# Graph attention with residual and layer norm: roots apart from scalings on POOL, Q or K ahead of three output projections, V ended in slot 4, transfers that change both quarters each time

## The chip, the core and the metric

The kernel runs on one core of one Trainium2 chip. The metric is the device time of one execution in microseconds (us), lower is better. Of the kernel before there are three timed executions and one profiled execution. "Same" means within 2% of the time before.

## What is computed

Eight batches of 1024 tokens with 384 features; six heads of 64 features; an adjacency matrix masks each score.

```python
q = _heads(x @ Wq + bq); k = _heads(x @ Wk + bk); v = _heads(x @ Wv + bv)
scores = einsum('bhqd,bhkd->bhqk', q, k) / sqrt(64)
probs  = softmax(scores + where(adj, 0.0, -9e15)[:, None], axis=-1)
ctx    = einsum('bhqk,bhkd->bhqd', probs, v)            # heads side by side: 384 features
x      = layernorm(x + (ctx @ Wf + bf), axis=-1)         # eps 1e-5
```

All arithmetic is float32. Projections and scores are made as three products of a high and a low part (`_hi`, `_lo`) of each operand.

## The kernel before

All engines run programs that were written out by hand and meet at semaphores. A batch is 24 **slots**, walked by all engines in the same order; PE (TensorE) may be a slot or more ahead. Slot s makes the scores of two heads for 128 queries: `group` of 256 queries s//6, pair of heads (s%6)//2, half s%2. Two slots fill one **group of probabilities** (12 a batch, numbered 0 to 11; group g is filled in slots 2g and 2g+1), which lies in half g%2 of `prob`.

What happens to a slot and a group:

- PE: `scores`, 12 matmuls (L499) into `score_ps`, as soon as DVE has read the slot before (`masked`).
- DVE (VectorE): `mask_scores` twice (L675, adds the mask and takes the row minimum into `row_min`), then `turn_squares` twice (L682, transposes 32x32 squares of `prob`), after ACT's exponentials. The first mask of a group waits until the transfers of the group two before have landed (`landed`), since they read the same half of `prob`. Then `divide` (L692) if the slot mixed a group, `invert_sums` in odd slots, and for each projected tile `add_residual` (L699) and `moments` (L706 to L716; the last one, L716, is the first guess of an inverse root, `guess_done`).
- ACT (ScalarE): an early eviction if the slot's first job is an "i", two exponentials (L605), then the other evictions. A Q or K job is read twice, as `q_hi`/`k_hi` and as `raw` (L597), which is one of two buffers; the next use of a `raw` buffer waits until POOL has made the low part out of it (`lo_done`).
- SP (SyncE): `move` in odd slots: after the transposes of a group it issues 16 transfers (L306), each of one quarter (32 partitions) of `prob` to one quarter of `prob_t`, 128 KB. The first eight, then a load of `x_in`, a store (`STORES`) and a load of `res` (`RES_LOADS`) if the tables say so, then the other eight, then a load of the adjacency.
- PE: `mix` (L514, 32 records) multiplies a landed group with V into `context_ps`.
- POOL (GpSimd): low parts (`low_part`, L793 and L789), masks out of the adjacency (L771), diagonals (`make_diagonal`, L799), `context_low` (L805), `residual` (L782: adds the bias to the loaded `res`), and `normalise`: 12 dependent operations on 128x2 (L820 to L823: three Newton steps of the inverse root) and then `scale_rows` (two operations on 128x384, L300). In a slot POOL does them in this order: low parts, mask, diagonal, context_low, residual, normalise.

`STEADY` names the jobs of PE in each slot behind the scores, as (kind, index, piece, ahead): "i" spreads inverse sums (L436), "m" mixes a group, "k", "q", "v" project (nine matmuls at L405 to L407), "x" transposes a piece of the next batch's x, "p" projects one tile of 128 tokens out (nine matmuls). A "p" waits until `context_lo` of the third mix of its group of queries is there (`context_lo_done`). The fourth number 1 marks work for the next batch; a negative index is work left from the batch before. Jobs other than "m" rotate over three PSUM banks. `RESIDUALS` and `NORMALISE` give the slots of POOL's work on each of the four groups of 256 tokens; -1 and -2 are the groups 3 and 2 of the batch before. The last batch has two more slots, 24 and 25.

Lines that the prediction speaks of: slot 21 is `[("p", 4), ("k", 1, 0)]`, slot 9 begins with `("p", 0)`, slot 5 is `[("v", 7), ("m", 0)]` where the mix of group 0 waits until the last V is evicted, and `NORMALISE = {0: -2, 8: -1, 12: 0, 18: 1}`.

Of the kernel before, what the change touches and what calls it, by code (L numbers as in the profile page):

```python
# [62 lines left out]

STORES = {1: -2, 9: -1, 13: 0, 19: 1}
RES_LOADS = {2: 0, 10: 1, 14: 2, 20: 3}
X_LOADS = {4: (0, 0), 6: (0, 1), 11: (1, 0), 12: (1, 1)}
RESIDUALS = {6: 0, 13: 1, 17: 2, 23: 3}
NORMALISE = {0: -2, 8: -1, 12: 0, 18: 1}

# [29 lines left out]
def evicted_early(mode, s):  # L99

    jobs = [w for w in slot_work(mode, s) if w[0] != "m"]
    return jobs[:1] if jobs and (jobs[0][0] == "i" or s == 5) else []

# [13 lines left out]
def graph_attention(nc, x, adj, wq, bq, wk, bk, wv, bv, wf, bf, out):  # L117
# [15 lines left out]
    with ExitStack() as ctx:  # L133
# [170 lines left out]
        def move_square(queue, group, a, c):  # L304

            queue.dma_start(prob_t[32 * c:32 * c + 32, group % 2, a].rearrange("p q h n -> p (q h n)"),  # L306
                            prob[32 * a:32 * a + 32, group % 2, c].rearrange("p q h n -> p (q h n)")
                            ).then_inc(landed[group % 2], 16)
# [6 lines left out]
        def _(sp):  # L315
# [26 lines left out]
            def move(b, group, part):  # L342
                if part == 0:
                    sp.wait_ge(squared, at(b, UNITS, 4 * group + 4))
                    sp.wait_ge(mixed, at(b, GROUPS, group + 1))
                for a in (2 * part, 2 * part + 1):
                    for c in range(4):
                        move_square(sp, group, a, c)

# [297 lines left out]
        def _(dve):  # L647
# [71 lines left out]
            def body(b):  # L719
                for s in slots_of(b.mode):  # L720
# [11 lines left out]
                    for job in work:  # L732
                        if job[0] == "p":
                            add_residual(b, job)
                            moments(b, job[1])

            weights = 0
# [27 lines left out]
        def _(pool):  # L765
# [41 lines left out]

            def normalise(b, group):
                pool.wait_ge(guess_done, at(b, 4, group + 1))
# [9 lines left out]
                for _ in range(NEWTON_STEPS):  # L819
# [3 lines left out]
                    result(nc.gpsimd.tensor_tensor(guess, guess, newton[:], ALU.mult))  # L823
                scale_rows(nc.gpsimd, group)

            def body(b):
                for s in slots_of(b.mode):
                    work = slot_work(b.mode, s)
                    for job in work:
# [9 lines left out]
                    for group in contexts_split(b.mode, s):  # L839
                        context_low(b, group)  # L840
                    if s in RESIDUALS:
                        residual(b, RESIDUALS[s])
                    if s in NORMALISE and (NORMALISE[s] >= 0 or b.mode != "first"):
                        normalise(b, NORMALISE[s])
                    if s == SLOTS:
                        normalise(b, 2)
                    if s == SLOTS + 1:
                        normalise(b, 3)

# [35 lines left out]
```

## Time and profile before

| | |
|---|---|
| median of 3 timed executions | 1355.2 us (1343.33, 1355.2, 1359.98) |
| the profiled execution's own time | 1353.83 us |
| its span, first to last instruction | 1352.0 us |
| mean granted clock of TensorE | 0.964 |
| busy: PE, weight loads, DVE, ACT, POOL | 89%, 66%, 78%, 54%, 48% |
| DMA queue of SP, share of 16 engines | 76.7% |

How to read it: PE is busy nearly nine tenths of the span, so the question at each change is which waits of PE it ends and what PE waits for then. An idle engine other than PE costs only where PE waits for it in the end. The timeline rows used below lie in the batch that begins at 346.14 us and ends at 507.96 us, the third of eight; slot numbers are those of that batch. In a timeline row the columns are start (us), length (us), engine, line, operation, what it writes and reads, its shape, how many were merged, and in brackets how long the engine was idle before it and what ended that.

### The profile page before, as it was taken

The numbers are of one execution on the slowest core, as the hardware profiler recorded it, in microseconds if no ns is written. First come the engines' busy times: TensorE is split into PE (matmuls) and PEld (weight loads), VectorE is DVE, ScalarE is ACT, GpSimd is POOL, SyncE is SP. The second block draws the span as 40 slices with busy tenths as digits, with TensorE's granted clock in tenths as the row PEclk, the third lists the DMA queues.
The fourth block names the chain that finished last, engine by engine and source line by source line (L and its number), as shares of the span: only waits on it lengthen the run. The fifth ranks groups of instructions, "written<-read, shape, count | busy, mean of one in ns | idle before, by whom it ended". The sixth has DMA issues, their size and how long they took to land.

```text
span 1352.0 us, 23753 instructions
## 1 busy us (share of the span) xinstructions
PE 1196.9 (89%) x8406; PEld 889.4 (66%) x8406; DVE 1057.4 (78%) x1617; ACT 736.7 (54%) x1404; POOL 654.4 (48%) x958
## 2 busy tenths in 40 slices
PE   7998899888998889888899898998899888998873
PEld 5765677656776667666677666766577666776542
DVE  5788777887778877788777888688877887779881
ACT  5655555555555656466455555555655555554540
POOL 1235562545625555375544664445643555624534
PEclk9999999998999999999898998999999999999987
DMA  4688867788678877788787887789867897678873
GB/s 154 161 190 213 189 159 191 190 221 192 153 190 199 223 181 177 184 207 201 170 199 173 212 191 183 177 188 224 193 152 190 199 228 185 162 170 196 204 185 86
DMA packets 111607, 251.66 MB, mean 186 GB/s; under 512 B 27904, under 2 KB 62336, under 8 KB 111488
## 3 DMA queue, kind: packets, MB, share of 16 engines
q1 hardware_dynamic: 111488, 250.13, 76.7%
q8 instruction: 67, 1.10, 0.4%
q14 instruction: 52, 0.43, 0.1%
HBM read 36.11 MB, written 12.58 MB: 36 GB/s over the span
## 4 chain that ended last, share of the span: by engine, by line
PE 51%; DVE 16%; SPq 11%; ACT 7%; POOL 7%; issue 5%; DMA 3%; POOLq 0%; ACTq 0%; DVEq 0%
PE context_ps L514 14%; PE score_ps L499 12%; SPq L306 10%; PE job_ps L405 8%; DVE prob L682 7%; PE job_ps L406 7%; PE job_ps L407 7%; ACT prob L605 5%; DVE prob L675 5%; DMA prob_t<-prob 2%; PE job_ps L436 2%; POOL res L300 2%; POOL context_lo L805 1%; POOL xt_lo L789 1%; DVE stats L706 1%
## 5 line engine op out<-in xcount | busy, mean ns | idle before, releaser
L675 DVE CUSTOM_DVE_ANT_0 prob<-score_ps,mask 128x1024 f32<-128x1024 f32 x384 | 454.5, 1220 | 169.0 <-PE score_ps L499 141.8
L605 ACT ACTIVATE prob<-prob,row_min 128x1024 f32<-128x1024 f32 x384 | 440.5, 1149 | 210.2 <-DVE row_min L675 210.1
L682 DVE STREAM_TRANSPOSE prob<-prob 128x1024 f32<-128x1024 f32 x384 | 458.5, 1232 | 75.9 <-ACT prob L605 75.9
L514 PE MATMUL context_ps<-prob_t,v_all 128*64 128x256 f32 x3072 | 356.5, 385 | 43.5 <-DMA prob_t<-prob 38.1
L514 PEld LDWEIGHTS context_ps<-prob_t,v_all 128*64 128x64 f32 x3072 | 232.7, 139 | 153.2 <-issue 60.1
L499 PE MATMUL score_ps<-k_hi,q_hi 64*128 64x512 f32 x768 | 141.6, 446 | 16.2 <-DVE row_min L675 16.2
L805 POOL TENSOR_TENSOR context_lo<-context,context_hi 128x256 fp32r<-128x256 f32 x96 | 70.6, 735 | 171.6 <-ACT context_hi L612 171.6
L771 POOL TENSOR_SCALAR mask<-adj_in 128x1024 f32<-128x1024 uint8 x64 | 67.0, 1046 | 170.8 <-DVE row_min L675 157.7
L793 POOL TENSOR_TENSOR q_lo<-raw,q_hi 128x256 fp32r<-128x256 f32 x95 | 69.3, 734 | 164.0 <-ACT raw L597 162.3
L405 PE MATMUL job_ps<-xt_hi,weight_hi 128*128 128x256 f32 (+1 forms) x423 | 143.3, 339 | 0.0
L406 PE MATMUL job_ps<-xt_lo,weight_hi 128*128 128x256 f32 (+1 forms) x423 | 138.4, 327 | 0.0
L407 PE MATMUL job_ps<-xt_hi,weight_lo 128*128 128x256 f32 (+1 forms) x423 | 138.1, 326 | 0.0
L405 PE MATMUL job_ps<-weight_hi,context_hi 128*128 128x384 f32 x192 | 77.1, 402 | 64.0 <-POOL context_lo L805 64.0
L499 PE MATMUL score_ps<-k_lo,q_hi 64*128 64x512 f32 x768 | 121.0, 392 | 0.0
L499 PE MATMUL score_ps<-k_hi,q_lo 64*128 64x512 f32 x768 | 120.5, 390 | 0.0
L612 ACT ACTIVATE context_hi<-context 128x256 fp32r<-128x256 f32 x96 | 40.1, 417 | 126.6 <-DVE context L692 126.6
L793 POOL TENSOR_TENSOR k_lo<-raw,k_hi 128x512 fp32r<-128x512 f32 x46 | 58.3, 1282 | 102.7 <-ACT raw L597 102.7
L300 POOL TENSOR_SCALAR res<-res,mean_var,inv_dev 128x384 f32<-128x384 f32 x64 | 105.0, 1647 | 3.5
L597 ACT ACTIVATE raw<-job_ps,bias_qk 128x256 f32<-128x256 f32 (+1 forms) x141 | 75.9, 538 | 56.2 <-POOL q_lo L793 32.6
L799 POOL TENSOR_TENSOR diag<-ident,inv_sum 128x512 f32<-128x512 f32 x96 | 100.0, 1042 | 10.5 <-DVE inv_sum L687 7.4
L499 PEld LDWEIGHTS score_ps<-k_hi,q_hi 64*128 64x128 f32 x768 | 57.7, 186 | 69.6 <-issue 36.4
L405 PEld LDWEIGHTS job_ps<-xt_hi,weight_hi 128*128 128x128 f32 x423 | 82.9, 196 | 21.3 <-issue 14.2
(72 smaller groups left out, 1700.9 us busy)
## 6 DMA issues: line engine op xcount, KB each, us to landing
prob_t<-prob SPq DMA_DIRECT2D x1536, 128.0 KB, 2.4
res<-in_x_dram SPq DMA_DIRECT2D x32, 384.0 KB, 3.9
out_dram<-res SPq DMA_DIRECT2D x32, 384.0 KB, 2.9
x_in<-in_x_dram SPq DMA_DIRECT2D x30, 384.0 KB, 3.8
adj_in<-in_adj_dram SPq DMA_DIRECT2D x31, 256.0 KB, 3.1
res<-in_x_dram SPq DMA_DIRECT2D x1, 768.0 KB, 6.7
prob_t<-in_L_gnn_Wk_dram SPq DMA_DIRECT2D x1, 576.0 KB, 4.0
prob_t<-in_L_gnn_Wq_dram SPq DMA_DIRECT2D x1, 576.0 KB, 8.1
```

Source lines behind the costliest of these rows:

```text
L300: engine.tensor_scalar(res[:, n, :], res[:, n, :], mean_var[:, group % 2, tile, 0:1], inv_dev[:, group % 2, tile:tile + 1], ALU.subtract, ...
L306: queue.dma_start(prob_t[32 * c:32 * c + 32, group % 2, a].rearrange("p q h n -> p (q h n)"), prob[32 * a:32 * a + 32, group % 2, c].rearr ...
L405: pe.matmul(dst, left_hi, right_hi, start=(t == 0), stop=False)
L406: pe.matmul(dst, left_hi, right_lo, start=False, stop=False)
L407: last = pe.matmul(dst, left_lo, right_hi, start=False, stop=(t == FT - 1))
L499: last[head] = pe.matmul(score_ps[:, head, keys], q_part[rows, pair, q], k_part[rows, pair, keys], start=(n == 0), stop=(n == 2))
L514: last = pe.matmul(context_ps[64 * head:64 * head + 64, 0:GQ], v_all[:, kt, col:col + HS], keys, start=(kt == 0), stop=(kt == TT - 1))
L605: nc.scalar.activation(probabilities(t), probabilities(t), ACT.Exp, scale=-1.0, bias=row_min[:, ring:ring + 1], accum_out=row_sum[:, s // ...
L675: nc.vector.tensor_tensor_reduce(probabilities(t), in_quarters(score_ps[:, head, :]), in_quarters(mask[:, s % 2, :]), 1.0, HUGE, ALU.add, ...
L682: nc.vector.transpose(probabilities(t), probabilities(t)).then_inc(squared, 1)
L793: nc.gpsimd.tensor_tensor(lo, copy[:, 0:width], hi, ALU.subtract).then_inc(lo_done, 1)
L799: nc.gpsimd.tensor_tensor(diag[:], ident[:].unsqueeze(1).to_broadcast([P, 4, P]), inv_sum[:, group % 2, :].unsqueeze(2).to_broadcast([P, 4 ...
```

## The change

- `normalise` is split: `find_root` (the 12 small operations) runs at the head of POOL's slot (`ROOTS`), ahead of the low parts; `scale_rows` stays at the end of the slot (`SCALINGS`), and that of group 1 moves from slot 18 to the end of slot 19. In the last batch the scaling of the last group is done by DVE.
- Slots 9, 15 and 21: the Q or K projection stands ahead of the output projection.
- V: two in slot 2, three in slot 3, three in slot 4; the spread of group 0 moves from slot 4 to slot 5.
- The residual of group 3 moves from slot 23 to slot 2 of the next batch, the load of its `res` from slot 20 to 22, the store of group 1 from slot 19 to 21.
- The 16 transfers of a group are issued along diagonals: each next one has another source quarter and another target quarter. Before, four in a row read the same source quarter.

```diff
 STEADY = {
...
-    5: [("v", 7, 0, 0), ("m", 0, 0, 0)],
+    5: [("i", 0, 0, 0), ("m", 0, 0, 0)],
...
-    21: [("p", 4, 0, 0), ("k", 1, 0, 1)],
+    21: [("k", 1, 0, 1), ("p", 4, 0, 0)],
...
-STORES = {1: -2, 9: -1, 13: 0, 19: 1}
-RES_LOADS = {2: 0, 10: 1, 14: 2, 20: 3}
+STORES = {1: -2, 9: -1, 13: 0, 21: 1}
+RES_LOADS = {2: 0, 10: 1, 14: 2, 22: 3}
 X_LOADS = {4: (0, 0), 6: (0, 1), 11: (1, 0), 12: (1, 1)}
-RESIDUALS = {6: 0, 13: 1, 17: 2, 23: 3}
-NORMALISE = {0: -2, 8: -1, 12: 0, 18: 1}
+RESIDUALS = {2: -1, 6: 0, 13: 1, 17: 2}
+ROOTS = {0: -2, 8: -1, 12: 0, 18: 1, 24: 2}
+SCALINGS = {0: -2, 8: -1, 12: 0, 19: 1, 24: 2}
...
-    return jobs[:1] if jobs and (jobs[0][0] == "i" or s == 5) else []
+    return jobs[:1] if jobs and jobs[0][0] == "i" else []
...
-                for a in (2 * part, 2 * part + 1):
-                    for c in range(4):
-                        move_square(sp, group, a, c)
+                for ahead in (2 * part, 2 * part + 1):
+                    for a in range(4):
+                        move_square(sp, group, a, (a + ahead) % 4)
...
+                    if s == SLOTS + 1:
+                        dve.wait_ge(root_ops, at(b, 4 * ROOT_OPS, 4 * ROOT_OPS))
+                        scale_rows(nc.vector, 3)
...
-                scale_rows(nc.gpsimd, group)
 
             def body(b):
                 for s in slots_of(b.mode):
+                    if s == SLOTS:
+                        residual(b, 3)
+                    if s in ROOTS and (ROOTS[s] >= 0 or b.mode != "first"):
+                        find_root(b, ROOTS[s])
                     work = slot_work(b.mode, s)
...
-                    if s in RESIDUALS:
+                    if s in RESIDUALS and (RESIDUALS[s] >= 0 or b.mode != "first"):
                         residual(b, RESIDUALS[s])
-                    if s in NORMALISE and (NORMALISE[s] >= 0 or b.mode != "first"):
-                        normalise(b, NORMALISE[s])
-                    if s == SLOTS:
-                        normalise(b, 2)
+                    if s in SCALINGS and (SCALINGS[s] >= 0 or b.mode != "first"):
+                        scale_rows(nc.gpsimd, SCALINGS[s])
                     if s == SLOTS + 1:
-                        normalise(b, 3)
+                        find_root(b, 3)
```

POOL in slots 18 to 20 of a middle batch, before: the end of the root of group 1 (three of its 12 operations), the scaling, the low parts of slot 19, the diagonal and low context of slot 20.

```order
L821 TENSOR_TENSOR newton<-newton,var_eps 128x2
L822 TENSOR_SCALAR newton<-newton 128x2
L823 TENSOR_TENSOR inv_dev<-inv_dev,newton 128x2
L300 TENSOR_SCALAR res<-res,mean_var,inv_dev 128x384 x2
L793 TENSOR_TENSOR q_lo<-raw,q_hi 128x256
L793 TENSOR_TENSOR k_lo<-raw,k_hi 128x512 x2
L799 TENSOR_TENSOR diag<-ident,inv_sum 128x512
L805 TENSOR_TENSOR context_lo<-context,context_hi 128x256
```

The same place now (line numbers are four higher for POOL and one higher for L300):

```order
L825 TENSOR_TENSOR newton<-newton,var_eps 128x2
L826 TENSOR_SCALAR newton<-newton 128x2
L827 TENSOR_TENSOR inv_dev<-inv_dev,newton 128x2
L793 TENSOR_TENSOR xt_lo<-raw,xt_hi 128x2x8x32 x2
L803 TENSOR_TENSOR diag<-ident,inv_sum 128x512
L809 TENSOR_TENSOR context_lo<-context,context_hi 128x256
L797 TENSOR_TENSOR q_lo<-raw,q_hi 128x256
L797 TENSOR_TENSOR k_lo<-raw,k_hi 128x512 x2
L301 TENSOR_SCALAR res<-res,mean_var,inv_dev 128x384 x2
L803 TENSOR_TENSOR diag<-ident,inv_sum 128x512
L809 TENSOR_TENSOR context_lo<-context,context_hi 128x256
```

The root went from behind slot 18's low parts to ahead of them, and the scaling from ahead of slot 19's low parts to behind them.

PE in slot 21, before: the last scores, then the output projection of tile 4 (nine matmuls, three shown), then K (nine, three shown).

```order
L499 MATMUL score_ps<-k_hi,q_lo 128x512 x4
L405 MATMUL job_ps<-weight_hi,context_hi 128x384
L406 MATMUL job_ps<-weight_lo,context_hi 128x384
L407 MATMUL job_ps<-weight_hi,context_lo 128x384
...
L405 MATMUL job_ps<-xt_hi,weight_hi 128x512
L406 MATMUL job_ps<-xt_lo,weight_hi 128x512
L407 MATMUL job_ps<-xt_hi,weight_lo 128x512
```

And now:

```order
L500 MATMUL score_ps<-k_hi,q_lo 128x512 x4
L406 MATMUL job_ps<-xt_hi,weight_hi 128x512
L407 MATMUL job_ps<-xt_lo,weight_hi 128x512
L408 MATMUL job_ps<-xt_hi,weight_lo 128x512
...
L406 MATMUL job_ps<-weight_hi,context_hi 128x384
L407 MATMUL job_ps<-weight_lo,context_hi 128x384
L408 MATMUL job_ps<-weight_hi,context_lo 128x384
```

Nine matmuls of K now stand between the scores and the projection that waits for `context_lo`. Slots 9 and 15 change in the same way with nine matmuls of Q (128x256).

## Rows read from the trace of the kernel before

**Rows 1.** The page, busy time of each engine, share of the span, instructions
```profile
PE 1196.9 (89%) x8406; PEld 889.4 (66%) x8406; DVE 1057.4 (78%) x1617; ACT 736.7 (54%) x1404; POOL 654.4 (48%) x958
```

**Rows 2.** Waits over the whole span: waiting <- awaited: us, times, longest
```profile
PE job_ps L405 <- POOL context_lo L805: 64.0, 25, 4.6
...
PE context_ps L514 <- DMA prob_t<-prob: 38.1, 20, 9.0
...
ACT raw L597 <- POOL q_lo L793: 32.6, 7, 4.9
...
DVE prob L675 <- DMA prob_t<-prob: 25.7, 17, 2.7
...
PE context_ps L514 <- ACT v_all L576: 5.4, 8, 0.7
```

**Rows 3.** Timeline of PE, slot 21
```profile
490.43 0.66 PE L405 MATMUL job_ps<-weight_hi,context_hi 128*128 128x384 f32 x1 [4.61 <-POOL context_lo L805]
...
493.44 0.52 PE L405 MATMUL job_ps<-xt_hi,weight_hi 128*128 128x512 f32 x1
...
495.79 0.73 PE L499 MATMUL score_ps<-k_hi,q_hi 64*128 64x512 f32 x4
```

**Rows 4.** Timeline of POOL, slots 18 to 20
```profile
472.68 2.54 POOL L789 TENSOR_TENSOR xt_lo<-raw,xt_hi 128x512 fp32r<-128x512 f32 x2 [2.08 <-ACT raw L595]
...
476.87 0.20 POOL L820 TENSOR_TENSOR newton<-inv_dev 128x2 f32<-128x2 f32 x1
...
480.22 3.28 POOL L300 TENSOR_SCALAR res<-res,mean_var,inv_dev 128x384 f32<-128x384 f32 x2
...
489.56 0.73 POOL L805 TENSOR_TENSOR context_lo<-context,context_hi 128x256 fp32r<-128x256 f32 x1 [1.89 <-ACT context_hi L612]
```

**Rows 5.** Timeline of ACT, slots 19 and 20
```profile
484.23 0.69 ACT L597 ACTIVATE raw<-job_ps,bias_qk 128x512 f32<-128x512 f32 x1 [4.91 <-POOL q_lo L793]
...
485.08 1.15 ACT L605 ACTIVATE prob<-prob,row_min 128x1024 f32<-128x1024 f32 x1
```

**Rows 6.** Timeline of DVE, slot 20
```profile
486.35 2.37 DVE L682 STREAM_TRANSPOSE prob<-prob 128x1024 f32<-128x1024 f32 x2 [3.76 <-ACT prob L605]
```

**Rows 7.** Windows: stretch, length, busy PE, PEld, DVE, ACT, POOL, clock, DMA share, GB/s
```profile
490.43:493.44 3.01, 3.01 (x9) 3.01 (x10) 2.85 (x4) 2.17 (x4) 0.00 (x0) 0.50 0.67 226
503.00:504.69 1.69, 1.69 (x12) 1.69 (x11) 1.58 (x3) 0.49 (x2) 0.74 (x1) 1.00 0.92 209
```

**Rows 8.** Timeline of PE, slot 9
```profile
412.01 0.66 PE L405 MATMUL job_ps<-weight_hi,context_hi 128*128 128x384 f32 x1 [2.56 <-POOL context_lo L805]
...
415.03 0.37 PE L405 MATMUL job_ps<-xt_hi,weight_hi 128*128 128x256 f32 x1
```

**Rows 9.** Timeline of SP, transfers of groups 3 and 5
```profile
402.40 10.04 SPq L306 DMA_DIRECT2D prob_t<-prob  x16
...
429.73 4.96 SPq L306 DMA_DIRECT2D prob_t<-prob  x8
...
435.37 5.62 SPq L306 DMA_DIRECT2D prob_t<-prob  x8
```

**Rows 10.** Timeline of PE, slot 14
```profile
443.26 3.67 PE L514 MATMUL context_ps<-prob_t,v_all 128*64 128x256 f32 x32 [1.74 <-DMA prob_t<-prob]
```

**Rows 11.** Timeline of SP, transfers of group 2
```profile
388.99 11.19 SPq L306 DMA_DIRECT2D prob_t<-prob  x16
```

**Rows 12.** Timeline of PE, slot 8, where group 2 is mixed
```profile
403.81 1.47 PE L514 MATMUL context_ps<-prob_t,v_all 128*64 128x256 f32 x12
```

**Rows 13.** DMA in 429 to 444 us: GB/s in 40 equal slices
```profile
GB/s 319 385 135 4 0 240 197 229 197 186 208 175 273 208 186 186 186 229 139 53 180 352 415 357 317 208 208 208 208 186 175 229 240 208 208 127 115 299 360 437
```

**Rows 14.** The page, DMA issues: count, KB each, us from issue to landing
```profile
prob_t<-prob SPq DMA_DIRECT2D x1536, 128.0 KB, 2.4
```

**Rows 15.** Timeline of POOL at the end of the program
```profile
1345.82 3.28 POOL L300 TENSOR_SCALAR res<-res,mean_var,inv_dev 128x384 f32<-128x384 f32 x2
```

**Rows 16.** Timeline of DVE at the end of the program
```profile
1339.06 0.56 DVE L699 TENSOR_TENSOR res<-job_ps,res 128x384 f32<-128x384 f32 x1 [3.24 <-PE job_ps L407]
```

More of the change, by code:

```diff
@@ L806, in context_low, with find_root @@
                                         ALU.subtract).then_inc(context_lo_done, 1)
-            def normalise(b, group):
+            def find_root(b, group):
                 pool.wait_ge(guess_done, at(b, 4, group + 1))
```

10 rows, old and new, of the table STEADY are left out of this document.

## The prediction

> **What bounds the kernel now.** I read the busy times first: PE is busy 89% of a span of 1352.0 us [rows 1], so about 155 us are PE's idle time or hidden in it, and the rest is work that this change only reorders. Then the waits [rows 2]: what PE waits for longest is `context_lo`, 64.0 us in 25 waits, three a batch; then 38.1 us for transfers that have not landed and 5.4 us for evicted V, 8 times 0.67 us. In the third batch the three waits for `context_lo` are 4.61 us in slot 21 [rows 3], 2.56 us in slot 9 [rows 8], and what is left of 64.0 / 8 = 8.0 us a batch, 0.8 us, belongs to slot 15. Each is a "p" job that stands first behind the scores. Behind the long ones TensorE runs at 1.2 GHz for a while: after 4.6 us of idling the nine matmuls of slot 21's projection took 3.01 us at a granted clock of 0.50, the same nine 1.69 us at 1.00 [rows 7]. Slot 9's nine took 415.03 - 412.01 = 3.02 us too [rows 8].
>
> Why is the low context of slot 20 late? Backwards: `context_lo` at 489.56 [rows 4] waits for the quotient that DVE makes after its transposes; these start at 486.35, 3.76 us after DVE had finished its masks, waiting for ACT's exponentials [rows 6]; these start at 485.08, behind an eviction to `raw` at 484.23 that had waited 4.91 us for POOL's `q_lo` [rows 5]. POOL was inside `normalise` for group 1: root from 476.87, scaling from 480.22 to 483.50 [rows 4], 6.6 us in one piece. ACT's wait of up to 4.9 us shows 7 times [rows 2], once in each batch that prepares a next one.
>
> **The change, part by part,** in that batch.
>
> *Slots 18 to 22.* The root takes 480.22 - 476.87 = 3.35 us. At the head of slot 18 it falls into POOL's 2.08 us of idling ahead of `xt_lo` [rows 4] and makes `xt_lo` at most 3.35 - 2.08 = 1.3 us later; the scaling (3.28) goes behind the low parts of slot 19. So `q_lo` comes 3.28 + 3.35 - 1.3 = 5.3 us earlier, and ACT's 4.91 us wait is gone. The exponentials are then held by DVE's masks, which had ended 3.76 us before the transposes began: transposes, quotient and `context_lo` come some 3.6 us earlier, and slot 21's wait of 4.61 shrinks to 1.0. The nine matmuls of K put ahead of it take 495.79 - 493.44 = 2.35 us [rows 3], more than that. The wait is gone whole: 4.61. With it goes the half clock: 3.01 - 1.69 = 1.3 for the projection and some 0.2 at the head of K, whose first matmul is still a slow one (0.52) [rows 3]. Together 6.1 us. What is queued behind the moved root is `xt_lo`, and PE's second K of slot 19 waits for it; it would be ready just as PE comes, so up to 0.5 us could be lost. I take 6.0.
>
> *Slot 9.* Nine matmuls of Q (128x256, half as wide as K, so about 1.2 us) fill part of the 2.56 us; `context_lo` itself hangs on DVE and does not come earlier. The rest, 1.3 us, stays. If the clock then stays at 2.4 GHz (my choice: an idling of 1.3 us instead of 2.56), another 1.3 is saved: 2.5. But slots 12 to 18 run at the pace of the transfers: the mix of group 5 waits for its landing [rows 10], and so does DVE's next mask, 25.7 us in 17 waits [rows 2]. That pace starts with group 5's transposes in slot 11, which come earlier by about 2.2, and group 4's landing lets through 1.5 to 2. I take 1.9.
>
> *Slot 15.* Q ahead hides the 0.8 us, but the next mix waits for group 6's landing, and it will wait that much longer: 0. What ends last there is the two-group loop transposes, 16 transfers, landing, mask.
>
> *V.* The last V is evicted a slot before the mix that needs it: 0.67 a batch [rows 2]. Slot 5's scores come some 1.2 us later: one V in (nine matmuls of 384 columns, 1.7 us as in [rows 7]), one spread out (four records of 256 columns, an eighth of the mix's 3.67 us [rows 10]). Group 2's transfers, issued from 388.99 to 400.18 [rows 11], land 2.4 us after the last issue's start [rows 14], at 402.0, and were mixed at 403.81 [rows 12]: slack 1.9 against 1.2 + 0.67. Just hidden; at worst 0.5 a batch is given back.
>
> *Moved residual, store and load.* The residual leaves POOL between slots 23 and 0, where the root now comes first; both fit before the first `q_lo` of slot 0. The store now stands in group 10's issues and not in group 9's: 0.6 us of SP's queue is moved. 0 in a middle batch.
>
> *Diagonal transfers.* 16 issues take 10.04 us [rows 9], 0.63 each, when SP is not held; a transfer lands 2.4 us after issue [rows 14]. Group 5 took 443.1 - 429.73 = 13.4 us to land, against 15 x 0.63 + 2.4 = 11.85. The issue pace stays, so only the 1.5 us of hold-up can go, in the three or four groups of a batch that PE and DVE wait for, and half of each counts, since a loop spans two groups: bounds 0 and 2.5 us a batch, 0 and 20 in all. While only these transfers run, the engines are 0.92 busy at 209 GB/s [rows 7]; the loads of x go through at 352 to 437 GB/s [rows 13], so something halves them. The targets alternated already, and that did not help, and the hold-up begins behind loads that the order does not touch. I take the low end, 0.3 a batch.
>
> The Trainium skill (SBUF — State Buffer, "Door 1: The DMA port swizzle") says that partitions 0 to 63 share eight of 16 ports and 64 to 127 the others, so a quarter reaches half the ports; by that, alternating halves could let two transfers run side by side, the case of the second rival. The same page ("Can I just issue two DMAs to hit both halves?") speaks against it: two such transfers gained only 6%. The trace has no pair that shows which.
>
> *Last batch.* No next batch, so the slot 18 to 22 term is absent. It keeps 1.9 of slot 9, some 1 to 2 from the store that leaves group 9's issues in a tail paced by landings, and at the very end DVE scales in POOL's place: two operations of at most 0.56 [rows 16] for 3.28 [rows 15], 2.1 saved. I take 6.
>
> **Sum.** 6.0 + 1.9 + 0.67 + 0.3 = 8.9 a batch, seven batches 62, and 6 for the last: 68. Less 2 for group 2's landing (0.3 a batch): 66. The profiled execution took 1353.8 us, so 1353.8 - 66 = 1288; it stands 1.4 below the median of the three runs, which themselves lie 17 us apart, so it is also the median's forecast within that spread.
>
> **Rivals.**
>
> *A. Half of it.* Another wait takes the place of slot 21's: `xt_lo` behind the late root holds K and with it ACT, so POOL's part brings nothing and only K's 2.3 us and Q's 1.2 are filled in, with half the clock's loss: 0.67 + 1.2 + 2.3 + 0.7 = 4.9, times 7, plus 4: 38, which gives 1316. For it: the root cannot start before the first guess, and DVE makes that only after slot 17's transposes. Against it: POOL idled 2.08 us right there. Chance 0.14.
>
> *B. The transfers' order pays as well.* Landings at their best, 2.5 a batch: 20 more, less the 2 already counted: 1270. Chance 0.13.
>
> *C. Slower.* Transfers that mix source and target quarters get in each other's way. A batch now takes 161.8 us for 12 groups, 13.5 each (507.96 - 346.14, the batch's bounds); with one or two other issues a group, a transfer of 0.63 would have to become 0.80 before the queue alone holds the old pace, and at 0.85 a batch is 12 x 14.4 = 173 us, 8 x 11.6 = 93 us more in all: 1447. For it: the engines are 0.92 busy already. Against it: each transfer alone touches the same quarters as before. Chance 0.03.
>
> *D. Within 2%.* Waits for landings grow to eat all but 20 us: 1334. Slots 12 to 18 show that PE's gains can be eaten so; against it, the 6.0 lie in slots 19 to 22, where groups 8 and 9 land with microseconds to spare. Chance 0.06.
>
> The forecast itself has 0.64, with 1276 to 1304 as its own range (last value of each term at its bounds, and the before runs' spread). 8 in 10 reaches into A and B: 1266 to 1314. A measurement tells 2% (27 us) from nothing; faster means below 1328. That takes in the forecast, B and nearly all of A: 0.64 + 0.13 + 0.12 = 0.89; within 2%: the rest of A and D, 0.08; slower 0.03.
>
> **What would show it.** Right: no wait of PE for `context_lo` in slot 21, 1.3 us in slot 9, none in slot 15 with the wait for the landing in slot 16 longer by as much; ACT's wait for `q_lo` gone; the total of that wait down from 64.0 to about 10 to 15 us; none for V; mean clock up. 16 issues still 10 us. Wrong: a wait of PE or ACT for `xt_lo` in slot 19 (A); 16 issues and landing near 11.9 in groups 5 to 7 (B); issues over 0.63 each with no load near (C).

## The result and the profile after

The changed kernel takes 1287.2 us (median of four executions, 1280.7 to 1288.7), the kernel before, in the same rounds, 1350.6 us (1343.3 to 1360.0): a ratio of 0.952, with a 95% interval of 0.945 to 0.958. In a second comparison below it was 1283.6 against 1349.6, again a ratio of 0.952. One of the six executions there, at a granted clock of 0.844, took 1339.5 us and is left out of both numbers. The profiled execution of the changed kernel took 1280.7 us, 6 below its median, and that of before 1353.8, some 3 above: what the two traces differ by (73 us) is more than the change is worth (63 us by the medians).

The page of the changed kernel: busy time of the engines, where [rows 1] answers, and the row on DMA issues, where [rows 14] answers.

```profile
PE 1177.3 (92%) x8406; PEld 867.3 (68%) x8406; DVE 1057.7 (83%) x1619; ACT 737.2 (58%) x1404; POOL 655.1 (51%) x956
...
prob_t<-prob SPq DMA_DIRECT2D x1536, 128.0 KB, 2.4
```

Its waits over the whole span, where [rows 2] answers (waiting <- awaited: us, times, longest).

```profile
PE context_ps L515 <- DMA prob_t<-prob: 39.8, 26, 3.6
...
DVE prob L676 <- DMA prob_t<-prob: 20.5, 16, 3.0
...
PE job_ps L437 <- DVE res L700: 12.8, 14, 1.4
PE job_ps L406 <- POOL context_lo L809: 12.5, 9, 1.9
```

PE's wait for the low context went from 64.0 us in 25 waits to 12.5 in 9. There is no row left for V nor for ACT's wait for `q_lo`. PE's busy time fell by 20 us with the same 8406 matmuls: fewer of them run at half the clock (mean granted clock 0.986 instead of 0.964). The wait for landed transfers stayed where it was, 39.8 us after 38.1.

PE in slot 21 of the third batch, which begins at 325.64 us in this trace; [rows 3] is the same place before.

```profile
462.25 0.51 PE L406 MATMUL job_ps<-xt_hi,weight_hi 128*128 128x512 f32 x1
...
464.48 0.33 PE L406 MATMUL job_ps<-weight_hi,context_hi 128*128 128x384 f32 x1
...
466.14 0.73 PE L500 MATMUL score_ps<-k_hi,q_hi 64*128 64x512 f32 x4
```

POOL in slots 18 to 21, where [rows 4] answers.

```profile
446.73 0.19 POOL L824 TENSOR_TENSOR newton<-inv_dev 128x2 f32<-128x2 f32 x1
...
450.06 2.55 POOL L793 TENSOR_TENSOR xt_lo<-raw,xt_hi 128x512 fp32r<-128x512 f32 x2
...
454.25 0.75 POOL L797 TENSOR_TENSOR q_lo<-raw,q_hi 128x256 fp32r<-128x256 f32 x1
...
457.76 3.29 POOL L301 TENSOR_SCALAR res<-res,mean_var,inv_dev 128x384 f32<-128x384 f32 x2
...
462.50 0.73 POOL L809 TENSOR_TENSOR context_lo<-context,context_hi 128x256 fp32r<-128x256 f32 x1 [0.45 <-ACT context_hi L613]
```

DVE's transposes of slot 20, where [rows 6] answers, and the window of slot 21's projection, where [rows 7] answers.

```profile
459.28 2.39 DVE L683 STREAM_TRANSPOSE prob<-prob 128x1024 f32<-128x1024 f32 x2 [0.16 <-ACT prob L606]
```

```profile
464.48:466.14 1.66, 1.66 (x12) 1.41 (x10) 1.50 (x4) 1.66 (x5) 0.00 (x0) 1.00 0.76 178
```

The root now runs ahead of `xt_lo`, `q_lo` is made before the scaling, and the transposes wait 0.16 us for ACT instead of 3.76. The low context is ready at 462.50 + 0.73 = 463.23 us, the projection that needs it starts at 464.48, behind K: 1.25 us in hand where 4.61 were missing. Its nine matmuls run at a granted clock of 1.00, in 1.66 us instead of 3.01.

Where the time went, stretch by stretch, is read from the starts of each slot's scores on PE, as means over the second to the seventh batch (worked out from the traces, us). The other kernels are those of the experiments below. Each column is one execution, so differences of a few tenths a batch are not sure; that of the changed kernel is one of its fastest, that of before one of its slower ones.

| slots | before | after | x1_rows | x3_same_halves | z1_p_first_9 | y1_one_piece | y3_before_split | y4_before_order |
|---|---|---|---|---|---|---|---|---|
| 0 to 9 | 61.66 | 60.75 | 61.14 | 61.12 | 60.82 | 60.86 | 61.75 | 61.87 |
| 9 to 10 | 8.60 | 6.38 | 6.38 | 6.38 | 7.96 | 6.39 | 7.68 | 6.39 |
| 10 to 15 | 31.21 | 32.13 | 34.94 | 34.81 | 30.33 | 32.37 | 31.44 | 32.30 |
| 15 to 18 | 16.97 | 15.61 | 15.57 | 15.75 | 17.03 | 15.80 | 17.14 | 16.78 |
| 18 to 22 | 32.34 | 26.69 | 26.71 | 26.67 | 26.17 | 29.26 | 27.27 | 28.38 |
| 22 to next | 12.17 | 12.17 | 12.17 | 12.18 | 12.17 | 12.51 | 12.18 | 12.48 |
| batch | 162.95 | 153.73 | 156.91 | 156.91 | 154.48 | 157.19 | 157.46 | 158.20 |

Before to after: 0.9 up to slot 9, 2.2 in slot 9, 0.9 given back up to slot 15, 1.4 up to slot 18, 5.7 up to slot 22. The first batch went from 159.4 to 147.2 us, the last from 191.9 to 185.0.

### The profile page after: what moved, and what is told of

The parts are those of the page before. It is cut to its first block, busy times and chain, and to the rows that moved or that the text cites. A ratio compares the mean times of both kernels' runs of the same rounds, so it can differ in the third digit from the quotient of the medians.

```text
span 1278.9 us, 23768 instructions
## 1 busy us (share of the span) xinstructions
PE 1177.3 (92%) x8406; PEld 867.3 (68%) x8406; DVE 1057.7 (83%) x1619; ACT 737.2 (58%) x1404; POOL 655.1 (51%) x956
## 4 chain that ended last, share of the span: by engine, by line
PE 53%; SPq 16%; DVE 16%; ACT 5%; issue 4%; DMA 3%; POOL 2%; DVEq 0%; POOLq 0%
PE context_ps L515 17%; SPq L307 15%; PE score_ps L500 13%; PE job_ps L406 7%; DVE prob L683 7%; PE job_ps L408 6%; PE job_ps L407 6%; ACT prob L606 5%; DVE prob L676 5%; DMA prob_t<-prob 3%; PE job_ps L437 2%; DVE res L700 1%; DVE stats L707 1%; POOL xt_lo L793 1%; SPq L370 1%
## 5 line engine op out<-in xcount | busy, mean ns | idle before, releaser
L515 PE MATMUL context_ps<-prob_t,v_all 128*64 128x256 f32 x3072 | 359.8, 388 | 40.0 <-DMA prob_t<-prob 39.8
L515 PEld LDWEIGHTS context_ps<-prob_t,v_all 128*64 128x64 f32 x3072 | 236.0, 140 | 151.3 <-issue 58.6
L500 PE MATMUL score_ps<-k_hi,q_hi 64*128 64x512 f32 x768 | 140.7, 444 | 10.5 <-DVE row_min L676 9.7
L407 PE MATMUL job_ps<-xt_lo,weight_hi 128*128 128x256 f32 (+1 forms) x423 | 135.5, 320 | 0.0
L408 PE MATMUL job_ps<-xt_hi,weight_lo 128*128 128x256 f32 (+1 forms) x423 | 135.5, 320 | 0.0
L301 POOL TENSOR_SCALAR res<-res,mean_var,inv_dev 128x384 f32<-128x384 f32 x62 | 101.9, 1650 | 0.0
L406 PEld LDWEIGHTS job_ps<-xt_hi,weight_hi 128*128 128x128 f32 x423 | 79.5, 188 | 32.3 <-issue 25.9
L797 POOL TENSOR_TENSOR k_lo<-raw,k_hi 128x512 fp32r<-128x512 f32 x46 | 58.8, 1288 | 74.5 <-ACT raw L598 74.4
L581 ACT ACTIVATE context<-job_ps 128x256 f32<-128x256 f32 x96 | 37.0, 386 | 95.4 <-PE job_ps L437 75.4
L408 PEld LDWEIGHTS job_ps<-xt_hi,weight_lo 128*128 128x128 f32 x423 | 79.6, 188 | 6.6
```

Source lines behind the costliest of these rows:

```text
L301: engine.tensor_scalar(res[:, n, :], res[:, n, :], mean_var[:, group % 2, tile, 0:1], inv_dev[:, group % 2, tile:tile + 1], ALU.subtract, ...
L406: pe.matmul(dst, left_hi, right_hi, start=(t == 0), stop=False)
L407: pe.matmul(dst, left_hi, right_lo, start=False, stop=False)
L408: last = pe.matmul(dst, left_lo, right_hi, start=False, stop=(t == FT - 1))
L500: last[head] = pe.matmul(score_ps[:, head, keys], q_part[rows, pair, q], k_part[rows, pair, keys], start=(n == 0), stop=(n == 2))
L515: last = pe.matmul(context_ps[64 * head:64 * head + 64, 0:GQ], v_all[:, kt, col:col + HS], keys, start=(kt == 0), stop=(kt == TT - 1))
```

## The experiments

Three comparisons, each on one chip with the kernel before beside it: 1349.6, 1348.1 and 1349.6 us. "After" is the changed kernel. How far a kernel lies from it is taken from the difference of the two ratios (0.001 is 1.35 us), since the kernels of the second and third comparison do not stand beside it; an interval of a ratio is 2 to 5 us to either side, so that a distance under 5 us is not shown.

### The order of the transfers

**x0_after_again** is the changed kernel unchanged, as the mark for the next three.

> The changed kernel as it is, on this job's chip, as the yardstick for the three others of the job. Both theories: the same ratio to the kernel before as measured already, 0.952, so 4.8% less.

Measured: 1283.6 us, ratio 0.952 (0.948 to 0.956).

**x1_rows**: the changed kernel with the old order of transfers.

```diff
-                for ahead in (2 * part, 2 * part + 1):
-                    for a in range(4):
-                        move_square(sp, group, a, (a + ahead) % 4)
+                for a in (2 * part, 2 * part + 1):
+                    for c in range(4):
+                        move_square(sp, group, a, c)
```

> The changed kernel with the transfers in the old order: four in a row read the same source quarter. My theory (the pace of SP's issues and the loads ahead set the landing, the order gives 0.3 us a batch): 2 to 4 us slower than the changed kernel, under 0.3%. Rival B (the order pays, up to 2.5 us a batch): 10 to 20 us slower, 0.8 to 1.6%, with the groups 5 to 7 landing 0.5 to 1.5 us later after their first issue. Issues stay 0.63 us apart in both.

Measured: 1299.5 us, ratio 0.963 (0.960 to 0.967): 15 us more than the mark. The order was worth far more than I gave it.

**x2_alternate**: each next transfer reads from the other half of the partitions (quarters 0 and 1 are one half, 2 and 3 the other). The writes change halves at six of the seven steps in the first eight and at five of seven in the other eight.

```diff
-                for ahead in (2 * part, 2 * part + 1):
-                    for a in range(4):
+                for ahead in (0, 2) if part == 0 else (1, 3):
+                    for a in (0, 2, 1, 3):
                         move_square(sp, group, a, (a + ahead) % 4)
```

> The changed kernel with transfers that change the half of the partitions (quarters 0 and 1 against 2 and 3) each time, sources 0, 2, 1, 3 and targets in step. If the halves are what matters (two transfers in flight then always use different halves), landings behind a load come earlier than with the diagonals: 3 to 8 us faster than the changed kernel. If the issue pace alone matters: within 2 us of it.

Measured: 1284.5 us, ratio 0.951 (0.947 to 0.954): 2 us below the mark by the ratios, 1 above it by the medians. No difference is shown, and the 3 to 8 us expected of it did not come.

**x3_same_halves**: eight in a row read from one half, and four in a row write to one half.

```diff
-                for ahead in (2 * part, 2 * part + 1):
-                    for a in range(4):
-                        move_square(sp, group, a, (a + ahead) % 4)
+                for c in ((0, 1), (2, 3)):
+                    for a in (2 * part, 2 * part + 1):
+                        for to in c:
+                            move_square(sp, group, a, to)
```

> The changed kernel with the worst order by halves: eight transfers read from one half, four in a row also write to the same half. If the halves matter: slower than the old order of rows, 5 us or more over the changed kernel, with more issues held over 0.65 us. If the issue pace alone matters: within 2 us of the old order.

Measured: 1310.6 us, ratio 0.971 (0.968 to 0.974): 26 us more than the mark, 10 more than x1_rows.

The place where it shows is group 5, whose landing the mix in slot 14 waits for. In the third batch, SP's issues around it and the mix, first of the changed kernel. (SP's rows: start, length, what is issued, how many. [rows 9, 10] are the same before.)

```profile
406.04 0.60 SPq L364 DMA_DIRECT2D res<-in_x_dram  x1
406.73 4.95 SPq L307 DMA_DIRECT2D prob_t<-prob  x8
...
420.24 3.67 PE L515 MATMUL context_ps<-prob_t,v_all 128*64 128x256 f32 x32 [2.41 <-DMA prob_t<-prob]
```

The same of x1_rows.

```profile
410.86 5.72 SPq L307 DMA_DIRECT2D prob_t<-prob  x8
...
425.82 4.54 PE L515 MATMUL context_ps<-prob_t,v_all 128*64 128x256 f32 x20 [3.15 <-DMA prob_t<-prob]
```

Of x3_same_halves.

```profile
410.96 5.32 SPq L307 DMA_DIRECT2D prob_t<-prob  x8
...
427.75 4.54 PE L516 MATMUL context_ps<-prob_t,v_all 128*64 128x256 f32 x20 [4.96 <-DMA prob_t<-prob]
```

And of x2_alternate.

```profile
410.67 4.95 SPq L307 DMA_DIRECT2D prob_t<-prob  x8
...
424.27 3.67 PE L515 MATMUL context_ps<-prob_t,v_all 128*64 128x256 f32 x32 [2.49 <-DMA prob_t<-prob]
```

From the group's first issue to the start of its mix: 13.5 us (420.24 - 406.73) after, 15.0 in x1_rows, 16.8 in x3_same_halves, 13.6 in x2_alternate. From the first issue to the last landing, as means of the second to the seventh batch: 13.6, 15.4, 16.0 and 13.4. The kernels below that keep the diagonal order have 13.6 to 14.6 there, so the two slow orders lie outside what one order gives from one execution to the next. In a late landing PE idles longer, and the mix that follows more often runs at the low clock. The window of that mix in x1_rows shows it.

```profile
425.82:432.44 6.62, 6.62 (x34) 4.03 (x34) 4.76 (x6) 2.38 (x4) 0.98 (x1) 0.55 0.95 256
```

It takes 6.62 us at a granted clock of 0.55, against 3.67 at 1.00 for the same 32 records in the changed kernel. Over the six batches the mix of group 5 starts 1.9 us later in x1_rows (96.44 against 94.57 from the batch's start) and takes 1.3 longer (6.09 against 4.77): the 3.2 us a batch of the table, part landing and part clock. By the ratios it is 15 / 8 = 1.9 a batch, since the profiled execution of the changed kernel was one of its fastest.

Which part of the order counts? Counted by halves, in x1_rows, x3_same_halves, after and x2_alternate the longest run of reads from one half is 8, 8, 2 and 1, that of writes to one half 2, 4, 2 and 2, and the times follow: 1299.5, 1310.6, 1283.6, 1284.5. So do the issues that took longer than 0.65 us, 88, 99, 78 and 69 of 1536. By this count runs of reads of 2 instead of 8 bring 15 us, and runs of writes of 4 instead of 2 cost 10. That the targets count is shown: x3_same_halves reads one quarter only twice in a row, where x1_rows reads it four times, and is slower all the same. That reads count by the half and not by the quarter is not shown: no run changes the source quarter each time and stays in one half.

The Trainium skill (SBUF — State Buffer, "Door 1: The DMA port swizzle") gives a reason for counting by halves, eight ports for each; these four runs agree with it, but no view shows the ports. Its other sentence there, that two DMAs on both halves gain only 6% ("Can I just issue two DMAs to hit both halves?"), tells nothing of sixteen queued ones behind other loads: here the landing of group 5 moved from 16.0 to 13.4 us with their order.

### Slots 18 to 22

**y1_one_piece**: root and scaling together again, at the end of slots 0, 8, 12 and 18.

```diff
-                    if s in ROOTS and (ROOTS[s] >= 0 or b.mode != "first"):
-                        find_root(b, ROOTS[s])
                     work = slot_work(b.mode, s)
...
-                    if s in SCALINGS and (SCALINGS[s] >= 0 or b.mode != "first"):
-                        scale_rows(nc.gpsimd, SCALINGS[s])
+                    if s in ROOTS and (ROOTS[s] >= 0 or b.mode != "first"):
+                        find_root(b, ROOTS[s])
+                        scale_rows(nc.gpsimd, ROOTS[s])
```

> The changed kernel with root and scaling in one piece at the end of slots 0, 8, 12 and 18, as before; all else as changed. My theory (the piece of 6.6 us in slot 18 holds ACT's eviction and through it exponentials, quotient and low context by 3.6 us): ACT waits some 4.9 us for q_lo in slot 19 again, slot 21's projection waits 2.4 us (3.6 less the 1.2 us that it has in hand behind K), so 2.4 to 4 us a batch with the slow clock, 17 to 28 us in all, 1.3 to 2.2% slower than changed. Rival (the reordering of K and p alone carries the gain): within 5 us of changed.

Measured: 1307.6 us, ratio 0.971 (0.967 to 0.975): 25 us more than x0_after_again. Of the 3.5 us a batch in the table 2.6 lie in slots 18 to 22. Its waits, and slot 21 of the third batch.

```profile
ACT raw L598 <- POOL q_lo L797: 32.8, 7, 5.0
...
PE job_ps L406 <- POOL context_lo L809: 27.2, 18, 2.3
```

```profile
468.20 0.69 ACT L598 ACTIVATE raw<-job_ps,bias_qk 128x512 f32<-128x512 f32 x1 [4.96 <-POOL q_lo L797]
...
474.40 0.66 PE L406 MATMUL job_ps<-weight_hi,context_hi 128*128 128x384 f32 x1 [2.34 <-POOL context_lo L809]
```

ACT's seven waits are back (32.8 us in all against 32.6), and with K ahead 2.34 us of the 4.61 remain in slot 21. The chain POOL, ACT, DVE, POOL, PE is shown.

**y2_p_first_21**: the changed kernel with the projection ahead of K in slot 21 again.

```diff
-    21: [("k", 1, 0, 1), ("p", 4, 0, 0)],
+    21: [("p", 4, 0, 0), ("k", 1, 0, 1)],
```

> The changed kernel with the output projection ahead of K in slot 21, as before. My theory: the low context is there 1.0 us after the scores end, so PE waits 1.0 us in slot 21 and nothing more: 7 us slower than changed, 0.5%. Rival (K's place carries the gain): the wait is 3 us or more and the clock falls, 25 us or more slower.

Measured: 1293.9 us, ratio 0.960 (0.956 to 0.963): 10 us more than x0_after_again. The wait in slot 21 is 1.03 to 1.05 us in each of the six middle batches; the prediction had it at 1.0. The nine matmuls behind it take 1.80 to 1.82: no half clock after any of these short waits. In its trace slots 18 to 22 take 27.88 us, 1.2 more than in the changed kernel; another 1.4 a batch lies in slots 10 to 15, at the landing of group 5, which this edit does not touch.

**y3_before_split**: the kernel before with the root apart from the scaling and the moved residual, store and load, and nothing else.

```diff
-STORES = {1: -2, 9: -1, 13: 0, 19: 1}
-RES_LOADS = {2: 0, 10: 1, 14: 2, 20: 3}
+STORES = {1: -2, 9: -1, 13: 0, 21: 1}
+RES_LOADS = {2: 0, 10: 1, 14: 2, 22: 3}
...
-RESIDUALS = {6: 0, 13: 1, 17: 2, 23: 3}
-NORMALISE = {0: -2, 8: -1, 12: 0, 18: 1}
+RESIDUALS = {2: -1, 6: 0, 13: 1, 17: 2}
+ROOTS = {0: -2, 8: -1, 12: 0, 18: 1, 24: 2}
+SCALINGS = {0: -2, 8: -1, 12: 0, 19: 1, 24: 2}
```

> The kernel before with only roots and scalings apart, and the residual, store and load of group 3 and 1 moved as changed; orders of PE's jobs and transfers as before. My theory: ACT's wait in slot 19 gone, slot 21's wait from 4.6 to 1.0 us and no half clock behind it: 5 us a batch, 35 us less than before (2.6%). Rival A (root at the head holds xt_lo, nothing gained by POOL's part): within 7 us of before.

Measured: 1316.4 us, ratio 0.977 (0.974 to 0.979): 31.6 us less than before. It is POOL's part, with the residual, store and load that moved along. Its waits:

```profile
PE job_ps L406 <- POOL context_lo L806: 40.1, 25, 2.6
...
PE context_ps L515 <- ACT v_all L577: 5.4, 8, 0.7
```

The waits for the low context fell from 64.0 to 40.1, 24 us in seven batches or 3.4 each (4.61 became about 1.0), and the longest is now 2.6, the one in slot 9. Of the 5.5 us a batch in the table 5.1 lie in slots 18 to 22 and 0.9 in slot 9, which this kernel does not touch (see the last section).

**y4_before_order**: the kernel before with Q or K ahead in slots 9, 15 and 21, and nothing else.

```diff
-    9: [("p", 0, 0, 0), ("q", 0, 2, 0), ("x", 0, 0, 1)],
+    9: [("q", 0, 2, 0), ("p", 0, 0, 0), ("x", 0, 0, 1)],
...
-    15: [("p", 2, 0, 0), ("q", 1, 3, 0)],
+    15: [("q", 1, 3, 0), ("p", 2, 0, 0)],
...
-    21: [("p", 4, 0, 0), ("k", 1, 0, 1)],
+    21: [("k", 1, 0, 1), ("p", 4, 0, 0)],
```

> The kernel before with only the Q or K projections ahead in slots 9, 15 and 21. My theory: slot 21's wait of 4.6 shrinks by K's 2.3 us with part of the slow clock, slot 9 brings 1.9, slot 15 nothing: 4.5 to 5.5 us a batch, 32 to 40 us less than before (2.4 to 3%). If it and y3 both give 35, their sum is more than the 62 that both together brought, since the wait in slot 21 is gone but once.

Measured: 1325.1 us, ratio 0.984 (0.981 to 0.987): 22.9 us less than before, and less than expected. (The profiles differ by 30 us; that of before is one of its slower executions.) In the table slot 9 gives its whole 2.2, but slots 10 to 15 take 1.1 of it back, and the last batch is 2.6 us longer than before. PE's waits show where it went. The first row is the low context, the second the landing.

```profile
PE job_ps L405 <- POOL context_lo L805: 27.2, 18, 2.3
```

```profile
PE context_ps L514 <- DMA prob_t<-prob: 55.4, 30, 9.0
```

36.8 us less for the low context, 17.3 more for landings than in [rows 2].

### Slots 9, 15, 12 and 18, and V

**z1_p_first_9**: the changed kernel with the projection first in slot 9 again.

```diff
-    9: [("q", 0, 2, 0), ("p", 0, 0, 0), ("x", 0, 0, 1)],
+    9: [("p", 0, 0, 0), ("q", 0, 2, 0), ("x", 0, 0, 1)],
```

> The changed kernel with the output projection ahead of Q in slot 9. My theory: PE waits 2.6 us instead of 1.3, and the clock falls again for the projection (1.3 us), but only 1.9 us a batch of these 2.6 reach the end since slots 12 to 18 go at the pace of the transfers: 15 us slower than changed, 1.2%. Rival (the transfers' pace swallows it all): within 4 us. Rival (all of it counts): 20 us.

Measured: 1288.5 us, ratio 0.955 (0.953 to 0.957), 3.5 us more than x0_after_again, with overlapping intervals; at 1.9 a batch it should have been 15. PE's two waits in the third batch:

```profile
390.38 0.41 PE L406 MATMUL job_ps<-weight_hi,context_hi 128*128 128x384 f32 x1 [2.55 <-POOL context_lo L809]
...
420.32 3.67 PE L515 MATMUL context_ps<-prob_t,v_all 128*64 128x256 f32 x32 [1.88 <-DMA prob_t<-prob]
```

The changed kernel has 1.29 us at the first place.

```profile
390.79 0.41 PE L406 MATMUL job_ps<-weight_hi,context_hi 128*128 128x384 f32 x1 [1.29 <-POOL context_lo L809]
```

So slot 9's wait is doubled, as it should be, and slot 10 starts 1.65 us later (means of the six batches). But the mix of group 5 starts only 0.94 later, and it ends 0.16 earlier, because it takes 3.67 us in all six batches instead of a mean of 4.77. From slot 15 to 18 the kernel loses 1.4, mostly in a wait for group 6 (1.23 instead of 0.13), and by the batch's end 0.75 is left. What slot 9 saves is taken back at the landings of groups 5 and 6, part as a wait, part as the low clock behind it.

**z2_p_first_15**: the same for slot 15.

```diff
-    15: [("q", 1, 3, 0), ("p", 2, 0, 0)],
+    15: [("p", 2, 0, 0), ("q", 1, 3, 0)],
```

> The changed kernel with the output projection ahead of Q in slot 15. My theory: PE waits about 0.9 us for the low context, and the wait for group 6's landing in slot 16 is shorter by as much: within 3 us of changed. Rival: 0.9 us a batch, 7 us slower, if group 6 has landed by the time PE comes.

Measured: 1288.9 us, ratio 0.954 (0.951 to 0.957): 3 us more, with overlapping intervals. Next to nothing, as the prediction had it.

**z3_v_as_before**: V in slots 2 to 5 as before, the spread of group 0 in slot 4.

```diff
-    2: [("i", -1, 0, 0), ("m", -1, 0, 0), ("v", 0, 0, 0), ("v", 1, 0, 0)],
-    3: [("v", 2, 0, 0), ("v", 3, 0, 0), ("v", 4, 0, 0)],
-    4: [("v", 5, 0, 0), ("v", 6, 0, 0), ("v", 7, 0, 0)],
-    5: [("i", 0, 0, 0), ("m", 0, 0, 0)],
+    2: [("i", -1, 0, 0), ("m", -1, 0, 0), ("v", 0, 0, 0)],
+    3: [("v", 1, 0, 0), ("v", 2, 0, 0), ("v", 3, 0, 0)],
+    4: [("i", 0, 0, 0), ("v", 4, 0, 0), ("v", 5, 0, 0), ("v", 6, 0, 0)],
+    5: [("v", 7, 0, 0), ("m", 0, 0, 0)],
...
-    return jobs[:1] if jobs and jobs[0][0] == "i" else []
+    return jobs[:1] if jobs and (jobs[0][0] == "i" or s == 5) else []
```

> The changed kernel with V in slots 2 to 5 and the spread of group 0 in slot 4, as before. My theory: the wait of 0.67 us for the last V is back in each of 8 batches and group 2 has a microsecond more in hand: 4 to 5 us slower than changed, 0.4%. Rival: less than 2 us, if the earlier V was paid for by a later landing of group 2.

Measured: 1292.1 us, ratio 0.957 (0.954 to 0.960): 7 us more, 0.9 a batch; the ends of the two intervals still overlap. The eight waits are back.

```profile
PE context_ps L515 <- ACT v_all L577: 5.4, 8, 0.7
```

**z4_q_first_11_17**: a step further on the same path. In slots 12 and 18 of the changed kernel PE waits for DVE to read the projection out of its bank (12.8 us in 14 waits), so Q goes ahead in slots 11 and 17 too.

```diff
-    11: [("p", 1, 0, 0), ("q", 1, 2, 0), ("x", 2, 0, 1)],
+    11: [("q", 1, 2, 0), ("p", 1, 0, 0), ("x", 2, 0, 1)],
...
-    17: [("p", 3, 0, 0), ("q", 2, 3, 0), ("x", 0, 1, 1)],
+    17: [("q", 2, 3, 0), ("p", 3, 0, 0), ("x", 0, 1, 1)],
```

> The changed kernel with Q ahead of the output projection in slots 11 and 17 as well. The next spread (slots 12 and 18) waits 0.65 and 1.3 us for DVE to read the projection's bank, three jobs back; with Q three jobs back it waits for ACT instead. If ACT is done by then: these waits go, 1.3 us of slot 18 counts (the mix of group 7 has landed), 0.65 of slot 12 does not (group 4 lands later): up to 10 us faster than changed, 0.8%. If the transposition of x behind it then waits for the same bank: within 2 us.

Measured: 1288.4 us, ratio 0.955 (0.953 to 0.956), no gain. PE's waits:

```profile
PE context_ps L515 <- DMA prob_t<-prob: 45.0, 24, 4.0
...
PE job_ps L416 <- DVE res L700: 2.5, 6, 0.4
```

The wait for DVE is nearly gone (2.5 us), and the wait for landings has grown from 39.8 to 45.0. It is the same lesson as in slot 9.

## Why the prediction came out right

The forecast was 1288 us and a gain of 66; measured were 1287.2 and 63.4. The total is right, but two of its terms were wrong and cancel: slot 9 stood (1.9 - 0.4) x 8 = 12 us too high, the order of the transfers (1.9 - 0.3) x 8 = 13 us too low. Nothing in the prediction tied the one to the other, so it is luck that the sum holds.

**Slots 18 to 22: right, 6.0 a batch.** The table has 5.65. The two ways of undoing it (25 us for POOL's part, 10 for PE's) add up to 35 us, 5 for each of seven batches. That is less than 5.65 since the two cover each other: without POOL's part 2.3 us of wait are left, without K 1.05, together 3.4 of the 4.61. The steps came as worked out: ACT's wait gone, 1.0 us left in slot 21 without K ahead, none with it, and the projection at the full clock. Two small costs were there as well: PE waits a mean 0.10 us for `xt_lo` in slot 19, for which up to 0.5 had been allowed, and 1.26 instead of 0.78 in slot 18 for DVE's read of a bank.

**Slot 9: the step that failed is how much group 4's and 5's landings let through.** The local saving was exactly as predicted: 1.29 us of wait left and full clock, 2.2 of 2.5 us in the stretch. But of the 1.9 that was to survive, z1_p_first_9 finds 3.5 / 8 = 0.4 a batch (0.75 in its profiled execution). Not 15 us, but 3.5, and even that is not clear of nothing. PE now waits a mean 0.59 us in slot 12 for group 4's landing, where before it waited for none, and 2.49 instead of 2.22 in slot 14 for group 5's. The prediction saw that slots 12 to 18 go at the transfers' pace and then took the upper end of what they would let through. It also missed the second way in which an early arrival at a late landing costs: after idling for 2.1 to 3.3 us ahead of the mix of group 5, PE ran it at the low clock in four of six batches (5.2 to 5.4 us instead of 3.67), before, after 1.7 to 2.9 us, in two of six. How long it idles does not decide it alone: the two at full speed came behind 2.41 and 3.30 us.

**The diagonal order: the term was 0.3 a batch, and it is 1.9.** 15 us by the ratios, three quarters of rival B's 20. The bounds of 0 and 2.5 held it; the choice of the low end was the error. Both reasons for it fail. "The targets alternated already, and that did not help" said nothing on the sources, and x3_same_halves shows that the alternating targets did help: without them it is 10 us worse. "The hold-up begins behind loads that the order does not touch" is true of where it begins, not of how long it lasts. And the change itself made the place tighter. SP's load of `res` before:

```profile
426.87 0.58 SPq L363 DMA_DIRECT2D res<-in_x_dram  x1
```

From its end, 426.87 + 0.58 = 427.45, SP stood still until group 5's first issue at 429.73 [rows 9], as a mean of six batches for 2.16 us; now it goes on from 406.04 + 0.60 = 406.64 at 406.73, directly behind the load. In the old order such a group takes 15.4 us to land in x1_rows and 14.4 in y4_before_order, instead of the 13.9 it took before, in the new one 13.6. So the two wrong terms belong together. In x1_rows the stretch from slot 10 to 15 is 3.7 us longer than before and eats nearly all that slots 0 to 9, 9 and 15 had saved (0.5 + 2.2 + 1.4 = 4.1); with the new order it is 0.9 longer. So the new order takes back most of what the earlier arrival costs at that landing; the saving of slot 9 itself it lets through only in small part, as z1_p_first_9 shows. What the order would be worth without the change of slot 9 is not known: no run has the old order, slot 9 as before and the rest as changed.

**V: right.** 0.67 a batch predicted, 0.9 measured, with an uncertainty as large (z3_v_as_before). The eight waits of 0.67 us are gone, and group 2's landing gave no new wait of PE in slot 8, so the 2 us set aside for it were not needed.

**Slot 15: right in size, wrong in detail.** Worth 0 predicted, 3 us measured, with overlapping intervals. The wait taken away was a mean 1.0 us rather than 0.8, in part since slot 21's 4.61 in the third batch is above its mean of 4.35. And the wait in slot 16 did not grow by as much: it fell, from a mean of 0.75 us to 0.13, since the slow mix of group 5 had already used up the time (in z1_p_first_9, where that mix is never slow, it is 1.23).

**Last batch:** 6 predicted, 191.9 - 185.0 = 6.9 in the profiles. **The base:** the sum started from the profiled 1353.8 us, while the medians of before in three further comparisons are 1348.1 to 1349.6. So the base was 3 us too high, and so was the gain, 66 against 63; this too cancels in the 1288.

**The rivals.** A did not happen: ACT does not wait for `xt_lo`, and PE only the 0.10 us in slot 19. B's worth came by three quarters, but not its sign: groups 5 to 7 land 13.6, 13.1 and 12.8 us after their first issue, not 11.9. Against the 13.9, 14.2 and 12.8 of before that is little; what the order is worth shows only beside x1_rows, since the other parts of the change had made the landings harder. D's mechanism, landings that eat what PE gains, is real, but with the old order it eats some 4 us a batch and leaves slots 18 to 22 alone, so that x1_rows still gains 50 us. C is refuted: an issue still follows the one before it after 0.63 us (sixteen with no load among them take 10.6 us on average, before 10.5) and the landings of groups 5 and 6 come sooner.

## What to carry to other kernels

Where a stage goes at the pace of transfers, price a saving ahead of it at nothing until something makes the landing itself earlier; test it by putting the wait back, not by reading that the wait is gone. A helper engine's long job should be split so that the part that others wait for goes first, and the whole chain behind the delay counted back to the bound engine: that was worth half of this change. And the order in which equal transfers are queued is free to choose: let no long run of them read from one half of the partitions, or write to one. Here that was worth a quarter of the change.

## What the runs showed of the hardware that was not expected

- **The order of quarter transfers alone moves this kernel by 26 us**, 1284.5 to 1310.6, at the same median issue pace of 0.63 us and the same bytes. Most of the difference comes between slots 10 and 15, at groups 4 to 6, among or just ahead of whose transfers loads of x and `res` stand; groups 8 and 9 land in 11.7 to 13.5 us in each of the four orders.
- **The same wait does not always bring the low clock.** Slot 9's projection after 2.55 us of idling, in the second to the eighth batch, took over 2.9 us in four of seven before, in two of seven in z1_p_first_9, in one of seven in y3_before_split, and 1.8 to 2.1 in the others. Two windows of z1_p_first_9 show both.

```profile
390.38:392.20 1.82, 1.82 (x11) 1.82 (x12) 1.65 (x3) 1.82 (x3) 1.82 (x2) 1.00 0.84 191
```

```profile
852.55:855.51 2.96, 2.96 (x10) 2.96 (x11) 2.79 (x4) 2.17 (x4) 2.96 (x2) 0.55 0.89 218
```

  What decides between the two stayed open. It is why y3_before_split gained 0.9 us in a slot that it doesn't touch, and it may be why executions of the changed kernel lie up to 9 us apart (1280.4 to 1289.6), which is not shown.
